# Causal attention of a two-layer block: F32R scores of two heads in the two row halves, and second products in pairs of key tiles

## The chip, the cores and the metric

One core of one Trainium2 chip (trn2) runs the whole program. The metric is device time in microseconds, 2697.65 us before the change as the median of three runs. TensorE is called PE in the rows (its weight loads PEld), VectorE DVE, ScalarE ACT, GpSimd POOL, and SP is the engine that issues most transfers.

## The reference, cut to what matters

Two layers, each `x + attention(norm(x)) * silu(ffn(norm(x)))`. The change touches the attention of the first layer and what feeds it. There x is (2, 2048, 256), with 16 heads of 16 dimensions:

```python
q = (x @ Wq.T).reshape(B, S, H, hd).transpose(0, 2, 1, 3)
...
def body(_, inp):
    qi, ci = inp
    scores = jnp.einsum('bhcd,bhsd->bhcs', qi, k) * scale
    qpos = ci * chunk + jnp.arange(chunk)
    mask = kpos[None, :] <= qpos[:, None]
    scores = jnp.where(mask, scores, jnp.finfo(scores.dtype).min)
    p = jax.nn.softmax(scores, axis=-1)
    return (None, jnp.einsum('bhcs,bhsd->bhcd', p, v))
```

The rest of the program (a mixture of experts, a second attention over windows and a second mixture of experts) is the same code in both kernels.

## The kernel before, in words

The program runs in stages, one block of all engines after the other: constants (`build_constants`), projection (`stage_project`), first attention (`stage_attention`), experts, join, windows.

**Constants.** GpSimd makes an identity, zeros, ones and two mask tiles (L116 to L139), one operation behind the other. The other engines wait for the end of this block.

**Projection** (L220 to L490). Eight chunks of 512 tokens. Per chunk VectorE normalises, TensorE transposes (L466) and multiplies (L457, F32R halves of inputs and weights), and q and k are cut into **three BF16 parts**: ScalarE takes the first (L425), VectorE the rest (L367), ScalarE the second (L430), VectorE the third (L372). SP stores them in DRAM as `qk_parts` (L308), 384 KB for each of four row tiles.

**Attention** (L579 to L912). A group is four heads of one of the two batch entries. There are eight groups, as a loop of three rounds of two, then two more written out. A group has four chunks c of 512 queries and, for chunk c, 4(c + 1) key tiles j of 128 keys; the last four of them lie on the diagonal and cover 512, 384, 256 and 128 queries. The steps, written out by `attention_steps` in one order that all engines follow, are:

- "A" (L721, L724, reduced at L859): the maxima. One product of 128 queries by up to 512 keys of one head, contraction 96 = 6 products of parts times 16 dimensions, into one bank of a ring of three; on the diagonal a mask product of an identity and a mask is added. VectorE reduces the bank to one maximum per query. There are 160 of these in a group. Half of them are made in the group before (in a head of their own for the first group), so the last group has only the other half.
- "M" (L866 to L870) cuts the negated maxima into three BF16 parts, "MT" (L731, L876) turns them into rows, and SP writes these into the operand `qa` of the scores (L691).
- "S" (L774, L777, exponential at L836): scores with keys on the partitions, contraction 99, the three more rows carrying the negated maximum. Two heads fill the two banks of a pair `pss`, and ScalarE takes both banks in one exponential of up to 1024 columns. On the diagonal a mask product is added. There are two `pss` pairs.
- "PV" (L792): the second products of one key tile, four heads in four column tiles of 32, float32 (each runs as two passes, so eight instructions), added up in `acc` over the key tiles. It comes after the scores of the next key tile.
- "COPY" (L844) and "O" (L802, L906, L909): sums to SBUF, four transposes through the ring, division, store.

`weave` (L533) sets the order: after each score it lets in as many maxima steps as keep both in step, so about one to one. The ring's wait in `a_step` is L720:

```python
wait(pe, ring_taken, r + 1 - RING)        # RING = 3
```

and the scores wait until the exponential two before is done (L773). In the head of the stage SP loads q and v, ScalarE issues the loads of k, and GpSimd fills the ones rows of `kb` (L660), clears the table `expert_in` (L665) and scatters the tokens into it (L668).

## Time and profile before

| what | value |
|---|---|
| three runs | 2697.65, 2702.26, 2695.6 us; median 2697.65 |
| the profiled execution | 2692.8 us, and its span is 2692.8 us |
| mean granted TensorE clock | 0.953 |
| projection | up to about 125 us |
| attention, its head | 133 to 224 us |
| attention, eight groups | 224 to 1157 us |
| experts, join, windows | 1157 to 2693 us |

The page has, for each engine, busy time and share of the span, then 40 slices of the span in tenths. A view of windows gives the busy time of each engine in a stretch, the granted clock there (1.00 is 2.4 GHz, 0.50 is 1.2 GHz) and the DMA share. The timeline lists instructions by start and duration, neighbours of one kind merged (x8 is eight of them). The duration of a product holds its latency too; what it keeps TensorE for is the distance from its start to the next start.

### The profile page before, as it was taken

Reading aid. Unit: us, or ns where it says so; the run is one execution under the profiler, and the core shown is the slowest. Engines: PE = TensorE matmul, PEld = TensorE weight load, DVE = VectorE, ACT = ScalarE, POOL = GpSimd, SP = SyncE. Lnnn points to the kernel's source line nnn. Section 1 sums busy time; section 2 is a strip of 40 time slices with the busy share of each in tenths; the row PEclk is TensorE's granted clock in tenths of the full one; section 3 lists DMA queues with packets and bytes.
Section 4 is the critical chain, followed back from the end, with each engine's and each line's share of the span. In section 5 each row is a group of like instructions: output and inputs, shape, how many; then the busy total and the mean of one; then the engine's idle time right before and its main releaser. Section 6 shows DMA issues by size and latency. Waiting matters only on the chain. (4 is left out here: it accounts for less than half of the span.)

```text
span 2692.8 us, 51134 instructions
## 1 busy us (share of the span) xinstructions
PE 2451.3 (91%) x16420; PEld 1589.0 (59%) x16420; DVE 1846.2 (69%) x3682; ACT 1406.8 (52%) x2776; POOL 815.1 (30%) x647
## 2 busy tenths in 40 slices
PE   5648999999999999969977599999999999999999
PEld 4512333333333333358866477777777777777777
DVE  7757877877787777424438476777667767766776
ACT  3404655656565566755634255555555555555554
POOL 1070000000000000014425355554455555444553
PEclk9858999999999999989988699999999999999999
DMA  4574041321404040033257000000000000000000
GB/s 135 191 170 65 5 62 26 41 52 16 61 6 62 6 60 5 7 127 133 102 177 241 18 13 12 11 13 13 13 13 13 9 11 13 13 13 13 13 9 9
DMA packets 189865, 132.85 MB, mean 49 GB/s; under 512 B 99857, under 2 KB 177687, under 8 KB 189712
## 3 DMA queue, kind: packets, MB, share of 16 engines
q1 hardware_dynamic: 160048, 100.06, 15.4%
q10 hardware_dynamic: 24160, 14.16, 2.2%
q0 software_dynamic: 5504, 16.69, 1.7%
q8 instruction: 83, 1.36, 0.2%
q14 instruction: 70, 0.57, 0.1%
HBM read 84.43 MB, written 46.14 MB: 48 GB/s over the span
## 5 line engine op out<-in xcount | busy, mean ns | idle before, releaser
L859 DVE TENSOR_REDUCE a_best<-a_ring 128x1 f32<-128x512 f32 (+3 forms) x1280 | 700.9, 604 | 214.0 <-PE a_ring L721 123.0
L836 ACT ACTIVATE a_probs<-a_pss 128x1024 f32<-128x1024 f32 (+3 forms) x640 | 554.0, 895 | 452.6 <-PE a_pss L777 228.7
L721 PE MATMUL a_ring<-a_kb,a_qa 96*128 96x512 bf16 (+3 forms) x1280 | 453.0, 365 | 67.2 <-DVE a_best L859 32.3
L774 PE MATMUL a_pss<-a_qa,a_kb 99*128 99x512 bf16 (+3 forms) x1280 | 433.9, 353 | 15.6 <-issue 7.2
L1771 ACT ACTIVATE w_probs<-w_pss,w_top 128x256 f32<-128x256 f32 x512 | 239.0, 476 | 379.7 <-DVE w_top L1859 365.0
L1606 POOL TENSOR_TENSOR w_probs<-w_probs,w_inv 128x512 f32<-128x512 f32 x256 | 301.0, 1176 | 395.7 <-DVE w_inv L1865 386.3
L962 POOL TENSOR_TENSOR e_w_r<-e_w,e_w_r 128x1024 fp32r<-128x1024 f32 x28 | 67.0, 2402 | 1032.7 <-ACT e_w_r L1035 1032.7
L1629 PE MATMUL w_psw<-wqkv,w_xr 128*128 128x512 f32 x1152 | 301.5, 398 | 11.6 <-POOL w_xr L1563 11.6
L774 PEld LDWEIGHTS a_pss<-a_qa,a_kb 99*128 99x128 bf16 x1280 | 123.5, 98 | 302.6 <-ACT a_probs L836 224.5
L792 PE MATMUL a_acc<-a_probs,a_vg 128*32 128x512 f32 (+3 forms) x2560 | 299.9, 541 | 0.1
L1669 PE MATMUL w_pss<-w_kd,w_qt 128*128 128x256 f32 x1536 | 278.4, 310 | 0.0
L1859 DVE TENSOR_REDUCE w_top<-w_pss 128x2 f32<-128x512 f32 x256 | 176.8, 691 | 141.5 <-PE w_pss L1669 140.7
L721 PEld LDWEIGHTS a_ring<-a_kb,a_qa 96*128 96x128 bf16 x1280 | 126.4, 99 | 223.9 <-DVE a_best L859 128.6
L1629 PEld LDWEIGHTS w_psw<-wqkv,w_xr 128*128 128x128 f32 x1152 | 205.6, 190 | 47.6 <-POOL w_xr L1563 12.1
L1669 PEld LDWEIGHTS w_pss<-w_kd,w_qt 128*128 128x128 f32 x1536 | 222.0, 195 | 4.1
L1629 PE MATMUL w_psw<-we,w_xr 128*128 128x512 f32 x768 | 204.2, 401 | 0.0
L1710 PE MATMUL w_pso<-w_pt,w_v 128*64 128x128 f32 x2048 | 168.3, 285 | 0.1
L1689 PE MATMUL w_pst<-identity,w_probs 128*128 128x128 f32 x1024 | 155.7, 275 | 0.0
L1629 PEld LDWEIGHTS w_psw<-we,w_xr 128*128 128x128 f32 x768 | 134.9, 188 | 22.9 <-issue 0.2
L1689 PEld LDWEIGHTS w_pst<-identity,w_probs 128*128 128x128 f32 x1024 | 123.6, 140 | 31.2 <-issue 5.7
L1882 DVE SCALAR_TENSOR_TENSOR w_y<-w_psw,coef,w_y 128x256 f32<-128x256 f32 x224 | 108.3, 484 | 42.4 <-PE w_psw L1629 23.2
L1710 PEld LDWEIGHTS w_pso<-w_pt,w_v 128*64 128x64 f32 x2048 | 106.5, 136 | 49.6 <-issue 49.1
(223 smaller groups left out, 3771.2 us busy)
## 6 DMA issues: line engine op xcount, KB each, us to landing
e_w<-in_w SPq DMA_DIRECT2D x16, 1024.0 KB, 7.9
qk_parts<-p_parts SPq DMA_DIRECT2D x32, 384.0 KB, 3.7
a_qa<-qk_parts SPq DMA_DIRECT2D x192, 64.0 KB, 2.5
a_kb<-qk_parts SPq DMA_DIRECT2D x42, 256.0 KB, 9.5
p_xin<-in_x SPq DMA_DIRECT2D x8, 512.0 KB, 5.4
v_rows<-p_vout SPq DMA_DIRECT2D x8, 512.0 KB, 5.1
a_vg<-v_rows SPq DMA_DIRECT2D x32, 128.0 KB, 9.1
expert_in<-zero POOLq DMA_DIRECT2D x16, 256.0 KB, 8.3
```

Source lines behind the costliest of these rows:

```text
L721: ins = pe.matmul(bank[:, 0:keys], qa[u][0:QR, i // TC, h, (i % TC) * P:(i % TC + 1) * P], kb[u][0:QR, h, k * CH:k * CH + keys], start=Tru ...
L774: ins = pe.matmul(pss[idx % 2][:, e, lo:CH], kb[u][0:MR, h, j * P:(j + 1) * P], qa[u][0:MR, c, h, lo:CH], start=True, stop=(j < TC * c))
L792: ins = pe.matmul(acc[32 * h:32 * h + 32, lo:CH], vg[u][:, j, h, :], probs[:, 2 * (pv % 2) + h // 2, h % 2, lo:CH], start=(j == 0), stop=( ...
L836: act.activation(probs[:, idx % 4, :, lo:CH], pss[idx % 2][:, :, lo:CH], ACT.Exp).then_inc(exp_done, 1)
L859: vec.tensor_reduce(best[:, i // TC, h * TC + i % TC, k:k + 1], bank[:, 0:keys], X, ALU.max).then_inc(ring_taken, 1)
L1606: pool.tensor_tensor(probs[:, p % 4, :, :], probs[:, p % 4, :, :], inv[:, :, p:p + 1].to_broadcast([P, 2, 2 * P]), ALU.mult).then_inc(p_re ...
L1629: ins = pe.matmul(psw[bank][:, :], xr[a][:, src, k, :], moving(b, k), start=(m == 0), stop=(m == len(pairs) - 1))
L1669: ins = pe.matmul(scores, qt[a][:, p, :], keys[b][:, p, :, :], start=False, stop=(a, b) == PARTS[-1])
L1689: ins = pe.transpose(pst[r % 2][:, 2 * e + role, :], probs[:, p % 4, e, role * P:(role + 1) * P], keep["identity"][:, :])
L1710: ins = pe.matmul(pso[e * DH:(e + 1) * DH, p % 4, :], v[(u + 1 + role) % 2][:, h * DH:(h + 1) * DH], pt[:, p % 2, 2 * e + role, :], start= ...
L1771: ins = act.activation(probs[:, p % 4, e, :], pss[p % 2][:, e, :], ACT.Exp, bias=top[:, e, p:p + 1], accum_out=rows[:, e, p:p + 1])
L1859: vec.tensor_reduce(top[:, :, p], pss[p % 2][:, :, :], X, ALU.max, negate=True).then_inc(top_ready, 1)
```

## The change

**q and k in two F32R parts.** VectorE's third part and ScalarE's second cast go; `parts` and `qk_parts` become 4 bytes wide with two parts. **Two heads in two row halves.** `qa` and `kb` hold head 2g at partitions 0 to 49 and head 2g + 1 at 64 to 113 (48 rows of products, 2 rows for the maximum), and steps "A" and "S" make two products each. An "A" step takes two banks of the ring, which keeps its three. **Masks.** The maxima's mask becomes two products of 64 rows for each head. The scores' mask goes; GpSimd sets the future's probabilities to zero behind the exponential, and the second product of a diagonal tile waits for that. **Order.** Every second key tile, the second products of two tiles come one behind the other, and `probs` holds four key tiles. The maxima are cut in two parts. The ones rows come by DMA from a constant tile.

```diff
-QR = 6 * HD
-MR = QR + 3
+QR = 3 * HD
+MR = QR + 2
+HALF = P // 2
...
+            for half, low_base in ((0, -HALF), (1, 0)):
+                for part, base in ((slice(0, P), low_base), (slice(0, HALF), HALF * half)):
+                    ch.link(pool.memset(keep["turn_halves"][part, half, :], 0.0))
+                    ch.link(pool.affine_select(out=keep["turn_halves"][part, half, :], in_=keep["turn_halves"][part, half, :],
...
+                    ch.link(pool.affine_select(out=keep["qk_halves"][part, half, :], in_=keep["zero16"][part, :],
...
+            ch.link(pool.memset(keep["ones32"][:, :], 1.0))
...
-                for m in range(4):
-                    rest_of(m)
-                for m in range(4):
-                    third(m)
+                for m in range(4):
+                    vec.wait_ge(high_part, 4 * c + m + 1)
+                    vec.scalar_tensor_tensor(out=parts[:, m, 1, :], in0=psq[m][:, :], scalar=HD ** -0.5 if m < 2 else 1.0,
+                                             in1=parts[:, m, 0, :].bitcast(F32), op0=ALU.mult, op1=ALU.subtract
+                                             ).then_inc(parts_ready, 1)
...
         for n, (c, j) in enumerate(pairs):
-            for h in range(GH):
-                steps.append(("S", c, j, h))
+            for g in range(GH // 2):
+                steps.append(("S", c, j, g))
...
-            if n:
-                pc, pj = pairs[n - 1]
+            for pc, pj in (pairs[n - 2], pairs[n - 1]) if n and n % 2 == 0 else ():
                 steps.append(("PV", pc, pj))
...
+KEPT = 4
...
+    in_ring = {"A": 2, "MT": 1, "O": 1}
...
-        qa = [st.sb(f"qa{u}", [MR, QC, GH, CH], BF16) for u in range(2)]
-        kb = [st.sb(f"kb{u}", [MR, GH, S], BF16) for u in range(2)]
+        qa = [st.sb(f"qa{u}", [P, QC, GH // 2, CH], F32R) for u in range(2)]
+        kb = [st.sb(f"kb{u}", [P, GH // 2, S], F32R) for u in range(2)]
...
-            for u in range(2):
-                pool.memset(kb[u][QR:MR, :, :], 1.0).then_inc(ones_set, 1)
...
+            for g, i, u, order in groups(pool):
+                idx = 0
+                for s in order:
+                    if s[0] == "S":
+                        _, c, j, hp = s
+                        if j >= TC * c:
+                            lo = (j - TC * c) * P
+                            pool.wait_ge(exp_done, primed + g * n_s + idx + 1)
+                            pool.tensor_tensor(spare[:, idx % spare.shape[1]:idx % spare.shape[1] + 1], keep["zero"][:, 0:1], keep["zero"][:, 0:1], ALU.add)
+                            block_probs = probs[:, idx % (KEPT * GH // 2), :, lo:lo + P]
+                            pool.affine_select(out=block_probs, in_=block_probs, compare_op=ALU.is_ge, fill=0.0, base=0,
+                                               pattern=[[0, 2], [1, P]], channel_multiplier=-1).then_inc(future_cleared, 1)
+                        idx += 1
...
+            def masked(bank, e, x, stop):
+
+                return pe.matmul(bank, keep["turn_halves"][half(e, HALF), x, :], keep["qk_halves"][half(e, HALF), x, :],
+                                 start=False, stop=stop)
...
-                wait(pe, ring_taken, r + 1 - RING)
-                ins = pe.matmul(bank[:, 0:keys], qa[u][0:QR, i // TC, h, (i % TC) * P:(i % TC + 1) * P],
-                                kb[u][0:QR, h, k * CH:k * CH + keys], start=True, stop=not diagonal)
+                wait(pe, ring_taken, r + 2 - RING)
+                for e in range(2):
+                    ins = pe.matmul(banks[e][:, 0:keys], qa[u][half(e, QR), i // TC, g, (i % TC) * P:(i % TC + 1) * P],
+                                    kb[u][half(e, QR), g, k * CH:k * CH + keys], start=True, stop=not diagonal)
+                    if not diagonal:
+                        ins.then_inc(ring_full, 1)
                 if diagonal:
-                    ins = pe.matmul(bank[:, keys - P:keys], keep["identity16"][:, :], keep["mask_qk"][:, :],
-                                    start=False, stop=True)
-                ins.then_inc(ring_full, 1)
+                    for x in range(2):
+                        for e in range(2):
+                            ins = masked(banks[e][:, keys - P:keys], e, x, x == 1)
+                            if x == 1:
+                                ins.then_inc(ring_full, 1)
...
+                        pe.wait_ge(exp_done, primed + g * n_s + max(idx - 1, 0))
+                        for e in range(2):
+                            ins = pe.matmul(pss[idx % 2][:, e, lo:CH], kb[u][half(e, MR), hp, j * P:(j + 1) * P],
+                                            qa[u][half(e, MR), c, hp, lo:CH], start=True, stop=True)
+                        ins.then_inc(s_ready, 1)
...
-                        pe.wait_ge(exp_done, primed + g * n_s + 2 * pv + 2)
+                        if j < TC * c:
+                            pe.wait_ge(exp_done, primed + g * n_s + GH // 2 * (pv + 1))
+                        else:
+                            pe.wait_ge(future_cleared, g * n_diagonal + GH // 2 * (j + 1))
...
+                for e in range(2):
+                    vec.wait_ge(ring_full, r + e + 1)
+                    vec.tensor_reduce(best[:, i // TC, e, g * TC + i % TC, k:k + 1], banks[e][:, 0:keys], X, ALU.max
+                                      ).then_inc(ring_taken, 1)
```

## Rows read from the trace of the kernel before

**Rows 1.** The page, part 1: busy us, share of the span, instructions, by engine.

```profile
PE 2451.3 (91%) x16420; PEld 1589.0 (59%) x16420; DVE 1846.2 (69%) x3682; ACT 1406.8 (52%) x2776; POOL 815.1 (30%) x647
```

**Rows 2.** Windows, the attention's groups: length, busy us by engine, clock, DMA share, GB/s.

```profile
225.00:1157.00 932.00, 889.79 (x6171) 336.81 (x6169) 701.46 (x1440) 569.05 (x672) 0.00 (x0) 0.99 0.21 32
```

**Rows 3.** Timeline, TensorE, first score of groups 0 and 2: start, us, what, idle.

```profile
223.60 0.63 PE L774 MATMUL a_pss<-a_qa,a_kb 99*128 99x512 bf16 x1
...
463.58 0.60 PE L774 MATMUL a_pss<-a_qa,a_kb 99*128 99x512 bf16 x1 [3.65 <-issue]
```

**Rows 4.** Timeline, TensorE, from one second product to the next in a full tile.

```profile
630.38 1.06 PE L792 MATMUL a_acc<-a_probs,a_vg 128*32 128x512 f32 x8
631.38 0.39 PE L774 MATMUL a_pss<-a_qa,a_kb 99*128 99x512 bf16 x1
...
632.16 0.38 PE L721 MATMUL a_ring<-a_kb,a_qa 96*128 96x512 bf16 x1
632.38 0.38 PE L774 MATMUL a_pss<-a_qa,a_kb 99*128 99x512 bf16 x1
...
633.30 1.06 PE L792 MATMUL a_acc<-a_probs,a_vg 128*32 128x512 f32 x8
```

**Rows 5.** Timeline, six reductions back to back, and two exponentials of two banks.

```profile
257.10 3.68 DVE L859 TENSOR_REDUCE a_best<-a_ring 128x1 f32<-128x512 f32 x6 [0.77 <-PE a_ring L721]
...
632.44 1.94 ACT L836 ACTIVATE a_probs<-a_pss 128x1024 f32<-128x1024 f32 x2 [1.02 <-PE a_pss L774]
```

**Rows 6.** Waits, 225 to 1157 us: who waited for whom, us in total, times, longest.

```profile
DVE a_best L859 <- PE a_ring L721: 119.4, 168, 4.1
PEld a_ring L721 <- DVE a_best L859: 84.9, 243, 0.8
```

**Rows 7.** Timeline, TensorE, chains of F32R products in the experts' stage.

```profile
1216.69 2.51 PE L1026 MATMUL e_psy<-e_w_r,e_hidden 128*128 128x256 f32 x19
...
1234.66 4.70 PE L1015 MATMUL e_psh<-e_rows_r,e_w_r 128*128 128x512 f32 x20
```

**Rows 8.** Groups by line and shape, reductions: count, busy us, mean ns, idle before.

```profile
L859 DVE TENSOR_REDUCE a_best<-a_ring 128x1 f32<-128x512 f32 x896 | 581.2, 684 | 171.4 <-PE a_ring L721 122.5 <-PE a_ring L724 36.4 <-remote 9.8
...
L859 DVE TENSOR_REDUCE a_best<-a_ring 128x1 f32<-128x384 f32 x128 | 70.5, 551 | 5.0 <-PE a_ring L724 4.0 <-PE a_ring L721 0.5
...
L859 DVE TENSOR_REDUCE a_best<-a_ring 128x1 f32<-128x128 f32 x128 | 36.1, 282 | 31.8 <-PE a_ring L724 26.9 <-remote 4.9
```

**Rows 9.** Timeline, TensorE, a float32 product whose weight load nothing covers.

```profile
2005.04 0.48 PE L1719 MATMUL w_psy<-wout,w_ot 128*128 128x256 f32 x1
```

**Rows 10.** Timeline, GpSimd, the constants' two masks.

```profile
3.05 0.29 POOL L126 TENSOR_SCALAR_AFFINE_SELECT mask_qk<-zero 128x128 bf16<-128x128 bf16 x1
3.49 0.29 POOL L128 TENSOR_SCALAR_AFFINE_SELECT mask_kq<-zero 128x128 bf16<-128x128 bf16 x1
```

**Rows 11.** Windows: before and behind a fall of the clock, one without, the head.

```profile
57.50:60.50 3.00, 1.38 (x11) 1.38 (x12) 2.54 (x12) 1.64 (x7) 0.00 (x0) 1.00 0.91 259
61.00:64.00 3.00, 3.00 (x12) 2.71 (x11) 3.00 (x6) 3.00 (x7) 0.88 (x1) 0.50 0.04 13
...
91.50:94.50 3.00, 1.49 (x13) 1.27 (x11) 2.62 (x17) 1.69 (x3) 0.00 (x0) 1.00 0.98 342
...
160.00:170.00 10.00, 8.92 (x30) 2.50 (x30) 9.34 (x22) 0.00 (x0) 0.51 (x1) 0.50 1.06 322
```

**Rows 12.** Timeline, TensorE, a maxima product of the head at the lower clock.

```profile
188.35 0.61 PE L721 MATMUL a_ring<-a_kb,a_qa 96*128 96x512 bf16 x1 [1.53 <-DVE a_best L859]
```

**Rows 13.** Groups by line, the projection's third part; windows, the projection.

```profile
L372 DVE TENSOR_TENSOR p_parts<-p_rest,p_parts 128x512 bf16<-128x512 f32 x32 | 19.9, 685 | 5.3 <-ACT p_parts L430 5.3
...
50.00:75.00 25.00, 21.21 (x115) 18.33 (x114) 23.60 (x75) 14.61 (x38) 2.09 (x2) 0.93 0.65 211
```

**Rows 14.** Windows, the head's first part, and the group of GpSimd's memset of the ones rows.

```profile
150.00:175.00 25.00, 20.68 (x77) 7.05 (x78) 21.98 (x51) 0.00 (x0) 13.80 (x22) 0.50 0.96 249
...
L660 POOL MEMSET a_kb<- 3x8192 bf16 x2 | 13.8, 6919 | 0.1
```

More of the change, by code:

```diff
@@ L236, in stage_project @@
         xnt = [[st.sb(f"xnt{r}_{u}", [P, KD, CH], F32R) for r in range(2)] for u in range(2)]
-        rest = st.sb("rest", [P, 4, CH])
-        parts = st.sb("parts", [P, 4, 3, CH], BF16)
+        parts = st.sb("parts", [P, 4, 2, CH], F32R)
         vout = st.sb("vout", [P, 2, TC, D])
@@ L420, in back, with high @@
             def back(c, n, u):
-                def first(m):
+                def high(m):
                     act.wait_ge(qk_ready, 4 * c + m + 1)
@@ L425, in first @@
                     act.activation(parts[:, m, 0, :], psq[m][:, :], ACT.Copy, scale=HD ** -0.5 if m < 2 else 1.0
-                                   ).then_inc(first_part, 1)
-                def second(m):
-                    act.wait_ge(rest_ready, 4 * c + m + 1)
-                    act.copy(parts[:, m, 1, :], rest[:, m, :]).then_inc(second_part, 1)
+                                   ).then_inc(high_part, 1)
                 def take_v(t):
@@ L440, in back @@
                 for m in range(4):
-                    first(m)
+                    high(m)
                 for t in range(TC):
                     take_v(t)
-                for m in range(4):
-                    second(m)
             chunks_skewed(act, front, back)
@@ L534, in weave @@
         pairs = [(c, j) for c in range(QC) for j in range(TC * (c + 1))]
-        total = sum(width(*p) for p in pairs) * GH
+        total = sum(width(*p) for p in pairs) * GH // 2
         ahead, steps, done, ahead_done, late = list(ahead), [], 0, 0, []
@@ L544, in advance @@
                 if u[0] == "MT":
-                    late.append([u, 6])
+                    late.append([u, 3])
                 else:
@@ L549, in weave @@
         for n, (c, j) in enumerate(pairs):
-            for h in range(GH):
-                steps.append(("S", c, j, h))
+            for g in range(GH // 2):
+                steps.append(("S", c, j, g))
                 done += width(c, j)
@@ L562, in weave @@
                     steps.append(("COPY", pc))
-                    late.append([("O", pc), 6])
-        c, j = pairs[-1]
-        steps += ahead + [u for u, _ in late] + [("PV", c, j), ("COPY", c), ("O", c)]
+                    late.append([("O", pc), 3])
+        c = pairs[-1][0]
+        steps += ahead + [u for u, _ in late] + [("PV", *p) for p in pairs[-2:]] + [("COPY", c), ("O", c)]
         return steps
@@ L624, in bank_of, with half @@
             return ring[(r_head + u * n_ring + r) % RING]
+        def half(e, rows):
+            return slice(HALF * e, HALF * e + rows)
         primed = 1
@@ L706, in _ @@
                     load(first, 1 - u)
-                for r, s in enumerate(s for s in order if s[0] in in_ring):
+                r = 0
+                for s in order:
                     if s[0] == "MT":
                         store_rows((u + s[1]) % 2, s[2], r_head + g * n_ring + r)
+                    r += in_ring.get(s[0], 0)
             for c in range(2):
@@ L741, in _ @@
                         chunk = s[3] // TC
-                        pe.wait_ge(first_q[chunk], 16 * len(parts_q))
-                    a_step(0, s, r, ring[r % RING])
+                        pe.wait_ge(first_q[chunk], 16 * q_loads)
+                    a_step(0, s, r, [ring[(r + e) % RING] for e in range(2)])
                 if s[0] == "MT":
@@ L875, in take_rows @@
                 wait(vec, m_landed[(c - 2) % QC], landed)
-                vec.tensor_copy(neg_rows[:, c % 2, :], bank[0:3 * GH * TC, 0:P // 2].bitcast(BF16)).then_inc(ring_taken, 1)
-            ch.link(vec.memset(neg_parts[:, :, :], 0.0))
+                vec.tensor_copy(neg_rows[:, c % 2, :], bank[0:2 * M, 0:P]).then_inc(ring_taken, 1)
+            for rest in range(2, P // M):
+                ins = vec.tensor_copy(neg_parts[:, rest, :], keep["zero"][:, 0:M])
+            ch.link(ins)
             r = 0
@@ L882, in _ @@
                 if s[0] == "A":
-                    take(s, r, ring[r % RING])
+                    take(s, r, [ring[(r + e) % RING] for e in range(2)])
                 elif s[0] == "M":
@@ L894, in _ @@
                     if s[0] == "A":
-                        take(s, at, bank)
+                        take(s, at, [bank_of(u, r + e) for e in range(2)])
                     elif s[0] == "M":
@@ L1942, in make_program @@
         }
-        build_constants(nc, keep)
         with ExitStack() as front:
-            keep["xn_all"] = Stage(nc, front).sb("xn_all", [P, NT, D])
+            early = Stage(nc, front)
+            for name in ("turn_halves", "qk_halves"):
+                keep[name] = early.sb(name, [P, 2, P], BF16)
+            keep["ones32"] = early.sb("ones32", [P, CH])
+            keep["xn_all"] = early.sb("xn_all", [P, NT, D])
+            build_constants(nc, keep)
             stage_project(nc, io, keep, dram)
```

169 lines of the change are left out of this document (82 added, 87 removed).

## The prediction

> **What bounds the kernel now.** I read the page first: TensorE is busy 91% of the span, VectorE 69%, ScalarE 52% [rows 1]. That is a mean over stages, so next the stage that the change touches, the attention from 225 us to 1157 us: TensorE 890 of 932 us, VectorE 701, ScalarE 569, GpSimd nothing [rows 2]. Two groups of heads take 463.58 - 223.60 = 240.0 us [rows 3]; later ones are a little slower, and I use **120.5 us a group**.
>
> Inside a group I take one key tile of full width apart. From one second product (L792) to the next is 633.30 - 630.38 = 2.92 us [rows 4]. Neighbouring starts give the prices: a 512-column score product holds TensorE for 0.22 us; from the second product to the next start it is 1.00 us, where 2 x 2 x 512 columns at 2.4 GHz are 0.85. So 8 x 0.22 + 1.00 = 2.76 us of the 2.92 are work; a switch between the two kinds costs 0.1 us behind the second product and, by what is left over, about as much in front of it. The tile is TensorE's. VectorE needs less but is close: six 512-wide reductions, one behind the other, take 3.68 us and one 0.68, so (3.68 - 0.68) / 5 = 0.60 us each [rows 5], 2.4 us for the four of a key tile. ScalarE: two exponentials in 1.94 us [rows 5] with 1.02 for one, 0.92 us each, two per tile. TensorE also waits 85 us on reductions, VectorE 119 us on TensorE [rows 6]: the two already trade turns over the ring of three banks.
>
> **Part 1, cheaper scores.** A score step becomes a pair: two heads in the two row halves, F32R, 512 columns. An F32R product of 512 columns comes every (4.70 - 0.40) / 19 = 0.226 us, one of 256 every (2.51 - 0.28) / 18 = 0.124 us [rows 7]; the price of a pair is not in the trace. Lower bound 0.23 us (both at once, as the four column tiles of L792 do: eight instructions in 1.06 us), upper 0.45 us (one after the other). I take 0.23, because the column tiles are the nearest row. A group has 17408 columns for each of two pairs, for scores and for maxima: 2 x (56 x 0.23 + 8 x (0.17 + 0.12 + 0.12)) = 32 us, where 4 x 17408 x 2 / 2.4 GHz = 58 us are spent now. The score mask (64 products, about 0.06 us each) goes, 3.7 us; the maxima's mask stays, 64 pairs of products of 64 rows, 4 us (bounds 4 and 8). The second products stay at 2 x 17408 x 2 columns, 29 us; with 20 blocks and not 40 the switches fall from 7.6 to 3.8 us. TensorE's own work falls from about 107 to about 73 us a group.
> The Trainium skill, "TensorE: Matmul & The Clock Gate", Part 3, says that products on distinct row groups run at the same time; by it the pair costs 0.23, without it 0.45, and no row here shows row halves.
>
> **Part 2, what it runs into.** VectorE keeps every reduction. In a group, with each width's busy time less the 0.084 us by which neighbours overlap [rows 8]: 112 x 0.60 + 16 x (0.467 + 0.332 + 0.198) = 83.2 us; the splits (three links of five remain, about 0.2 us each), the turned rows and the outputs add 5.5: **88.7 us**. So VectorE is the bound, and every wait of its counts.
> The Trainium skill, "TensorEngine Tiling (Array Packing)", PSUM Bottleneck, speaks against the change in the same way: a faster array leaves the emptying of PSUM as the limit. By that alone the group would be 89 us; the rest is this kernel's order.
>
> *The ring.* There are still three banks, but a maxima step now takes two. It may start when the first reduction of the pair before is done; now it may start with two reductions still ahead of it. From the end of that reduction: about 0.05 us of signal, 0.10 us of weight load that nothing covers (0.48 for a product behind a pause [rows 9] against 0.38 in a stream [rows 4]), 0.39 us of product, 0.04 us of signal: 0.58, against 0.52 that the second reduction covers. That is 0.07 us per full pair; behind a narrow reduction (0.2 to 0.47 us) or with mask products (0.16 more) it is 0.1 to 0.5. Over the 48 plain and 32 masked pairs: 14.6 us a group.
>
> *The second products in pairs.* TensorE is in order: from the last maxima pair (load 0.10, columns 0.21, switch 0.09) through two second products (3 x 0.43 + 0.55 = 1.84), score pair (0.33) and the next maxima pair's 0.43 are 3.0 us, in which VectorE has 1.73 us of work. Stall 1.2 us instead of 0.07. Twelve full blocks, four of 512 + 384 (0.95), four of 256 + 128 (0.15): 18.9 us. Two blocks fewer switches do not help VectorE; the single block of now stalls it by less, since its cover is longer.
>
> *Group end.* No maxima follow the last 512 + 384 block; then come narrow scores, GpSimd's clearing of the last tiles, copy and turn: 5 us of stall.
>
> Sum, at full clock: 88.7 + 14.6 + 18.9 + 5 = **127 us** against 120.5, +6.5.
> ScalarE: 4 x 0.92 = 3.7 us in a period of two full key tiles, which takes 8 x 0.60 + 3 x 0.07 + 1.28 = 6.3 us: covered. GpSimd's clearing after the exponential: 0.29 us for 128 columns [rows 10], 0.3 to 0.5 for 256, plus a small add; two score pairs pass before the product that needs it, so nothing, except at the group end, where it is counted. The wait on it stands in TensorE's queue ahead of the next scores, so if it were late, all would be.
>
> **Part 3, the clock.** In such a period TensorE streams, between two blocks of second products, one maxima and one score pair every 1.27 us; by the busy time of a row, (0.23 + 0.39) / 1.27 = 49%. The granted clock fell to 1.2 GHz behind a stretch with TensorE busy 1.38 of 3 us, and stood behind one with 1.49 [rows 11]. The maxima ahead of the first group ran at 1.2 GHz although TensorE was busy 8.92 of 10 us [rows 11]. So the clock would fall again and again, and come back only by the blocks of second products, 3.6 us without a pause at 1.2 GHz. What it costs there, per period: a 512-column product takes 0.61 us from load to end [rows 12] and not 0.39, so a maxima turn is 1.5 us, three of them 4.5, and the turn over a block is 0.43 + 0.09 + 3.41 + 0.2 + 0.43 = 4.6 us: 9.1 and not 6.3 us. Seventeen periods are 155 us, the extras outside full periods 20 us as at full clock (127 - 17 x 6.3), and some 8 more for turns over narrow reductions: 183 us a group. I take two fifths of the groups' time at the low level (ends: none and all; an estimate, since both the falls and the returns need their stretch to come by): 0.6 x 127 + 0.4 x 183 = **149 us**.
>
> **Part 4, in front.** The projection loses the third part: 32 x 0.60 us of VectorE and a cast of ScalarE [rows 13]. VectorE was busy 23.6 of 25 us there, with 75 instructions, of which a chunk has 36: 11.6 to 12 us a chunk; without 2.4 it is 9.2 to 9.6, and TensorE with 24 x 0.23 + 24 x 0.12 + 8 x 0.11 = 9.4 plus small waits takes over: 9.9. Seven chunks x 1.7 and 2 at the end: -13 us. The stores grow from 384 to 512 KB but in longer rows; as covered as before. The constants gain eleven operations of GpSimd at some 0.4 us apiece (3.49 - 3.05 [rows 10]) in the block that all engines wait for: +4.5 us. The head: VectorE busy 22 of its first 25 us [rows 14]. 13.8 us of GpSimd memset ahead of the table's clearing go [rows 14], so GpSimd's scatter ends earlier; against it stand 43 pairs with turns at 1.2 GHz (0.3 to 0.6 us each). Net 0, bounds -15 and +20. Loads of q and k have the same bytes and number, in rows twice as long; four row stores in place of three, and four stores of ones in SP's queue ahead of the values, lie behind the wait for k.
>
> **Sum.** 7 x (149.4 - 120.5) = +202; the last group, whose second half has no maxima, +12; front -13 + 4.5 + 0: +205. From the profiled execution, 2692.8 us (its span is its time), 2898; the median shown is 4.9 us above it: **2900 us**.
>
> **The rivals.** (a) *The clock holds.* For it: the stretch of 1.49 of 3 us, as busy as I expect here, did not lower it. 7 x 6.5 + 3 - 9 = +40: 2740 us. (b) *The row halves do not run side by side* (the change doesn't do what it says): TensorE is busier, so the clock holds, but each block's stall grows by 0.46 us, 16 blocks, 7.4 us a group: 2790 us. (c) *Faster.* TensorE waits less than I think: if the weight load is pulled ahead of the ring's wait and the mask products add nothing, ring stalls fall to 4 us and the block stalls to 13.4: 111 us a group, 7 x -9.5 - 9 - 5 = -80: 2620 us. It decides as soon as the two stalls together are under 27 us (I have 33.5) and the clock stays up; for it: TensorE's work does fall by a third, and VectorE waits 119 us now that a freer TensorE could serve. (d) *Low clock throughout*: 7 x 62.5 + 25 = +460: 3155 us.
>
> **Chances.** Clock falling often 0.43 (with (d) 0.03 more), (a) 0.20, (b) 0.12, faster (c and between) 0.18, no change 0.04. A measurement can tell 0.3% here, 8 us. Slower 0.78, same 0.04, faster 0.18. The range takes in (a), (b) and most of the clock case's bounds (one tenth to two thirds low), and leaves out the far end of (c) and (d): 2650 to 3060. The forecast case's own range is 2780 to 3060.
>
> **What would show it.** VectorE as busy in the attention as before in us, with waits on the ring's products of about 1.2 us at each block of second products; ring waits of TensorE far above 85 us; a granted clock that swings between 1.0 and 0.5 in the attention; score pairs starting within some ns of each other, 0.23 us from pair to pair; projection chunks of 10 us. A group under 120 us at full clock would show my turns wrong; a steady clock would leave (a).

## The result, and the profile after

| | before | after |
|---|---|---|
| median of the compared runs | 2696.62 us (2693.27 to 2702.26) | 3012.43 us (3007.04 to 3017.72) |
| profiled execution, its span | 2692.8 us | 3006.5 us |
| mean granted clock of the span | 0.953 | 0.849 |

The ratio is 1.1165, with a 95% interval of 1.1142 to 1.1188: slower by 316 us, inside the range, and 112 us above the forecast of 2900. A run over 1.5% above the fastest of its kernel counts as slow and is left out of comparisons; this befell three of e9's six runs and four of e11's seven. The page of the changed kernel, part 1 and the clock's row of part 2, against [rows 1]:

```profile
PE 2563.3 (85%) x16420; PEld 1650.7 (55%) x16420; DVE 1846.2 (61%) x3591; ACT 1392.2 (46%) x2744; POOL 941.8 (31%) x1168
...
PEclk9755978777676777667799877999999999999999
```

VectorE's busy time is the same to a tenth of a us by chance: the projection lost its third parts, and in the seven groups cut out below VectorE shows 15 us more. TensorE has less to do in the attention and still shows 112 us more busy time, since its products ran at the lower clock for much of it: slices 6 to 20, attention but for the end of the last, stand at 6 to 8. To see where the 314 us of the two spans lie, I cut both at the first exponential of a group: the head, seven groups, the last group. Windows of the kernel before (columns as in [rows 2]):

```profile
151.20:225.84 74.64, 43.43 (x139) 13.20 (x140) 46.76 (x98) 0.00 (x0) 39.78 (x48) 0.50 0.55 158
225.84:1061.02 835.18, 796.55 (x5519) 304.96 (x5517) 653.31 (x1344) 498.92 (x588) 0.00 (x0) 0.99 0.23 34
1061.02:1154.20 93.18, 91.23 (x638) 30.72 (x636) 46.63 (x94) 69.51 (x83) 0.00 (x0) 1.00 0.03 7
```

The same windows of the changed kernel:

```profile
144.00:237.26 93.26, 36.95 (x178) 16.80 (x178) 47.12 (x93) 0.00 (x0) 31.47 (x32) 0.50 0.50 133
237.26:1336.44 1099.18, 896.88 (x5518) 353.71 (x5518) 668.47 (x1291) 500.36 (x588) 120.75 (x448) 0.74 0.17 25
1336.44:1466.70 130.26, 108.83 (x596) 38.88 (x596) 47.02 (x88) 69.50 (x83) 16.34 (x62) 0.70 0.02 5
```

The stretch ahead of the head is 7.2 us shorter, the head 18.6 us longer, seven groups 264.0 us longer (157.0 us each and not 119.3), the last group 37.1, and what follows 1539.8 us and not 1538.6: 11.4 + 264.0 + 37.1 + 1.2 = 313.7 us. A clock of 0.74 means that (1 - 0.74) x 2 = 52% of the groups' time was at the lower level. The waits of the attention, 225 to 1467 us, against [rows 6]:

```profile
PEld a_ring L740 <- DVE a_best L883: 363.9, 442, 1.6
DVE a_best L883 <- PE a_ring L740: 228.1, 247, 5.4
DVE a_best L883 <- PE a_ring L730: 193.2, 164, 4.2
PE a_ring L740 <- DVE a_best L883: 190.6, 391, 1.1
```

TensorE and VectorE now wait for each other far more than before (TensorE's weight loads 364 us, where it was 85), and neither is full. The timeline of one stretch at full clock shows both sides of it. TensorE:

```profile
416.71 0.39 PE L740 MATMUL a_ring<-a_kb,a_qa 48*128 48x512 f32 x2
416.94 0.40 PE L797 MATMUL a_pss<-a_qa,a_kb 50*128 50x512 f32 x2
417.89 0.50 PE L740 MATMUL a_ring<-a_kb,a_qa 48*128 48x512 f32 x2 [0.55 <-DVE a_best L883]
418.22 0.39 PE L797 MATMUL a_pss<-a_qa,a_kb 50*128 50x512 f32 x2
419.17 0.50 PE L740 MATMUL a_ring<-a_kb,a_qa 48*128 48x512 f32 x2 [0.55 <-DVE a_best L883]
...
420.44 0.44 PE L740 MATMUL a_ring<-a_kb,a_qa 48*128 48x384 f32 x2 [0.55 <-DVE a_best L883]
420.73 0.29 PE L730 MATMUL a_ring<-qk_halves,turn_halves 64*128 64x128 bf16 x4
420.94 1.92 PE L814 MATMUL a_acc<-a_probs,a_vg 128*32 128x512 f32 x16
422.80 0.44 PE L797 MATMUL a_pss<-a_qa,a_kb 50*128 50x384 f32 x2
```

VectorE in the same stretch:

```profile
417.14 4.93 DVE L883 TENSOR_REDUCE a_best<-a_ring 128x1 f32<-128x512 f32 x8 [2.69 <-PE a_ring L740]
423.51 0.69 DVE L883 TENSOR_REDUCE a_best<-a_ring 128x1 f32<-128x512 f32 x1 [1.44 <-PE a_ring L740]
```

A pair of 512 columns holds TensorE for 416.94 - 416.71 = 0.23 us. A maxima pair comes every 1.28 us, in which TensorE stands 0.55. Then comes the block of sixteen second products, and VectorE, which had run through eight reductions, stands for 1.44 us.

Two maxima turns and a block at the lower clock, which lasted from 599.8 to 606.7 us, VectorE:

```profile
600.87 1.29 DVE L883 TENSOR_REDUCE a_best<-a_ring 128x1 f32<-128x512 f32 x2 [0.28 <-PE a_ring L740]
602.44 1.29 DVE L883 TENSOR_REDUCE a_best<-a_ring 128x1 f32<-128x512 f32 x2 [0.29 <-PE a_ring L740]
607.09 3.12 DVE L883 TENSOR_REDUCE a_best<-a_ring 128x1 f32<-128x384 f32 x5 [3.35 <-PE a_ring L730]
```

A turn takes 602.44 - 600.87 = 1.57 us here, the turn over a block 607.09 - 602.44 = 4.65, and the wait behind the block is 3.35 us. Windows around one fall, a return and the next fall:

```profile
422.40:425.80 3.40, 2.50 (x22) 1.14 (x14) 2.29 (x4) 2.40 (x4) 1.30 (x6) 0.99 0.01 1
425.80:429.20 3.40, 3.40 (x18) 0.59 (x16) 1.57 (x3) 0.20 (x1) 0.85 (x3) 0.50 0.00 0
429.20:432.60 3.40, 2.12 (x20) 1.05 (x16) 1.66 (x3) 2.60 (x4) 1.06 (x4) 1.00 0.01 2
432.60:442.80 10.20, 9.48 (x50) 4.43 (x54) 7.14 (x14) 4.57 (x5) 0.00 (x0) 0.50 0.01 2
```

Here the clock falls behind a stretch with waits (TensorE busy 2.50 of 3.40 us), comes back behind one in which TensorE never stands (a block of second products at 1.2 GHz), and falls again behind the next pauses.

### The profile page after: what moved, and what is told of

It is laid out like the page before. It is cut to its first block and busy times, and to the rows that moved or that the text cites. A ratio compares the mean times of both kernels' runs of the same rounds, so it can differ in the third digit from the quotient of the medians.

```text
span 3006.5 us, 51095 instructions
## 1 busy us (share of the span) xinstructions
PE 2563.3 (85%) x16420; PEld 1650.7 (55%) x16420; DVE 1846.2 (61%) x3591; ACT 1392.2 (46%) x2744; POOL 941.8 (31%) x1168
## 5 line engine op out<-in xcount | busy, mean ns | idle before, releaser
L883 DVE TENSOR_REDUCE a_best<-a_ring 128x1 f32<-128x512 f32 (+3 forms) x1280 | 721.2, 606 | 486.5 <-PE a_ring L740 236.6
L740 PE MATMUL a_ring<-a_kb,a_qa 48*128 48x512 f32 (+3 forms) x1280 | 351.6, 546 | 265.5 <-DVE a_best L883 213.1
L814 PE MATMUL a_acc<-a_probs,a_vg 128*32 128x512 f32 (+3 forms) x2560 | 412.5, 780 | 7.2 <-POOL a_probs L670 7.2
L668 POOL TENSOR_TENSOR a_spare<-zero 128x1 f32<-128x1 f32 x256 | 49.4, 193 | 1130.7 <-ACT a_probs L858 1130.0
L740 PEld LDWEIGHTS a_ring<-a_kb,a_qa 48*128 48x128 f32 x1280 | 151.3, 233 | 452.4 <-DVE a_best L883 396.2
L797 PE MATMUL a_pss<-a_qa,a_kb 50*128 50x512 f32 (+3 forms) x1280 | 317.0, 503 | 23.9 <-ACT a_probs L858 14.2
L797 PEld LDWEIGHTS a_pss<-a_qa,a_kb 50*128 50x128 f32 x1280 | 146.6, 229 | 217.7 <-issue 181.4
L814 PEld LDWEIGHTS a_acc<-a_probs,a_vg 128*32 128x32 f32 x2560 | 85.0, 141 | 205.6 <-issue 146.3
```

Source lines behind the costliest of these rows:

```text
L740: ins = pe.matmul(banks[e][:, 0:keys], qa[u][half(e, QR), i // TC, g, (i % TC) * P:(i % TC + 1) * P], kb[u][half(e, QR), g, k * CH:k * CH ...
L797: ins = pe.matmul(pss[idx % 2][:, e, lo:CH], kb[u][half(e, MR), hp, j * P:(j + 1) * P], qa[u][half(e, MR), c, hp, lo:CH], start=True, stop ...
L814: ins = pe.matmul(acc[32 * h:32 * h + 32, lo:CH], vg[u][:, j, h, :], probs[:, GH // 2 * (pv % KEPT) + h // 2, h % 2, lo:CH], start=(j == 0 ...
L883: vec.tensor_reduce(best[:, i // TC, e, g * TC + i % TC, k:k + 1], banks[e][:, 0:keys], X, ALU.max).then_inc(ring_taken, 1)
```

## The experiments

The theory: a group at full clock takes 127 us, since VectorE waits over each long block and turns with TensorE over three banks; the waits bring the clock down, and the clock makes the rest. The rival of each run is that the part in question costs nothing. Each run stood beside the kernel before on one of four chips, where that took 2671 to 2674 us; the changed kernel was run again in the same way (e5), and the variants are to be compared with that, 3000.5 us. A variant changes the stage of attention alone.

**e1, one tile of second products at a time.**

```diff
-            for pc, pj in (pairs[n - 2], pairs[n - 1]) if n and n % 2 == 0 else ():
+            for pc, pj in (pairs[n - 1],) if n else ():
```

> Undoes one part of the change: the second products of a key tile come alone, behind the scores of the next tile, as before; all else as changed. Theory (VectorE's waits behind TensorE's blocks of second products, and a clock that falls because TensorE is idle between them): the pause between blocks is half as long, VectorE waits about 0.45 us at each block of a full tile and not 1.2 us at each pair, and the clock stays up for more of the time; a group falls from 157 us to about 130 us, the whole to about 2820 us (2760 to 2900). Rival (the pairing is a gain, since it saves half of the switches, and the loss lies elsewhere, in the ring or in GpSimd's clearing): 20 switches more a group at 0.19 us, so 3010 + 30 = 3040 us.

2863.86 us, ratio 1.0704 (1.0669 to 1.0739), clock 0.872. The time is in the theory's range: the pairing costs 137 us in this kernel. The groups got less of it than expected, 143.5 us each at a clock of 0.77 and not about 130.

**e2, each score pair issued twice.** The second issue writes the same numbers into the same bank: work for TensorE and nothing else.

```diff
-                        for e in range(2):
+                        for e in [e for _ in range(2) for e in range(2)]:
                             ins = pe.matmul(pss[idx % 2][:, e, lo:CH], ...
```

> The changed kernel, but each pair of score products is issued twice into the same banks, so that TensorE has 80 x 0.2 us more to do in a group and the result is the same. Theory (the low clock is most of the loss and comes from TensorE's idle time): TensorE is busy for more of the time between blocks, the clock stays up in most of the attention, mean clock of the groups 0.9 or more against 0.74, a group about 133 us against 157, and the kernel gets faster by more work: about 2850 us (2770 to 2930). Rival (the loss is VectorE's waits in the order of the steps, the clock only goes along): each stall at a block grows by 0.23 us, 16 x 0.23 = 4 us a group, 3010 + 30 = 3040 us, and the same clock.

2880.8 us, ratio 1.0777 (1.0738 to 1.0817), clock 0.913. Added work makes the kernel 120 us faster. The seven groups:

```profile
210.15:1228.56 1018.41, 877.10 (x6638) 409.53 (x6638) 667.88 (x1290) 504.63 (x588) 120.68 (x448) 0.88 0.18 27
```

145.5 us a group at 0.88, where the theory had 133 at 0.9 or more. VectorE and ScalarE did what they did without it, and nothing was taken away, so it is the clock that gives the time back. It gives back 120 of the 327 us by which e5 is over the kernel before.

**e3, each maxima product waits for its own bank,** and its mask products stand right behind it, so that the first of a pair need not wait until two banks are free.

```diff
-                wait(pe, ring_taken, r + 2 - RING)
                 for e in range(2):
+                    wait(pe, ring_taken, r + e + 1 - RING)
...
+                    if diagonal:
+                        for x in range(2):
+                            ins = masked(banks[e][:, keys - P:keys], e, x, x == 1)
+                    ins.then_inc(ring_full, 1)
```

> Undoes the two-bank wait alone: each product of a maxima step waits for its own bank of the ring, with its own mask products behind it. Theory (a maxima step that takes two of three banks leaves VectorE's turn uncovered, 14.6 us a group, and makes each block's stall longer): the ring's stalls nearly go, those at blocks fall from 1.2 to about 1.0 us; at full clock 127 - 17 = 110 us a group; with half of the time at the low clock, about 138 us against 157: 2880 us (2820 to 2940). Rival (the first product goes out in time and only the row halves' running together counts): the two heads' products no longer start together and TensorE loses what the halves gave, no gain or a loss: 3010 to 3050 us.

2856.57 us, ratio 1.0686 (1.066 to 1.0713), clock 0.876. The wait for two banks costs 144 us. Of these, 17 lie in the head of the attention, where the first exponential comes at 193.91 us, and at 211.18 in e1, whose head is the changed kernel's; the groups take 143.0 us at 0.78.

**e4, both.**

> Both: second products tile by tile, and a wait for each bank. Theory: VectorE's reductions are the bound with few stalls, TensorE is busy evenly enough for the clock to stay up; 105 to 112 us a group against 120.5 of the kernel before, so faster than before: 2696 - 7 x 12 = about 2610 us (2560 to 2700). Rival (GpSimd's clearing and the load of the F32R weights set the pace): not under the kernel before, 2750 to 2850 us.

2811.32 us, ratio 1.0557 (1.0499 to 1.0615), clock 0.889: the theory missed, by 200 us. The two repairs overlap (137 + 144, together 189 us). The groups say what is left over:

```profile
195.53:1144.81 949.28, 882.61 (x5520) 384.01 (x5519) 649.40 (x1290) 496.17 (x588) 123.25 (x451) 0.81 0.20 31
```

135.6 us a group at 0.81. They range from 129.3 us at 0.87 to 146.9 at 0.71; a line through the seven gives 120 us at full clock and 0.32 us more for each us at the lower level (an estimate; the same line for e5 gives 128 and 0.36). So at full clock this order would, by that line, be as fast as the kernel before (119.3 us), and no faster, though TensorE's work fell by a third by the prediction's count. Its timeline at full clock shows part of the reason, TensorE:

```profile
292.18 1.06 PE L810 MATMUL a_acc<-a_probs,a_vg 128*32 128x512 f32 x8
...
293.99 0.40 PE L740 MATMUL a_ring<-a_kb,a_qa 48*128 48x512 f32 x1
294.69 0.50 PE L740 MATMUL a_ring<-a_kb,a_qa 48*128 48x512 f32 x1 [0.31 <-DVE a_best L879]
295.12 1.07 PE L810 MATMUL a_acc<-a_probs,a_vg 128*32 128x512 f32 x8
```

VectorE in the same stretch, and a window of 12 us:

```profile
293.95 2.48 DVE L879 TENSOR_REDUCE a_best<-a_ring 128x1 f32<-128x512 f32 x4
...
299.58 3.17 DVE L879 TENSOR_REDUCE a_best<-a_ring 128x1 f32<-128x512 f32 x6 [0.54 <-PE a_ring L740]
...
292.00:304.00 12.00, 11.26 (x79) 4.90 (x78) 10.01 (x22) 6.94 (x8) 0.00 (x0) 1.00 0.01 3
```

A key tile takes 295.12 - 292.18 = 2.94 us. VectorE does not stand in this one: four reductions of 0.60 us and 0.54 us of splits are as long. But the last maxima product waits 0.31 us for a bank, the block begins only behind it, and the two products of that pair (293.99 and 294.69) no longer start together. Over the 12 us VectorE stands 2.0 us in all, 0.24 to 0.70 at a time, behind blocks and mask products. How much each of these costs was not measured.

**e5, the changed kernel again.**

> The changed kernel as it is, beside the variants, to have a second reading of it. Its first execution had VectorE and TensorE standing for 10.5, 5.9 and 3.1 us at a time in the head of the attention, and its first exponential at 237 us, where the variant with the scores twice, which has the same head, had it at 210 us. Theory (that was of the one execution, the clock is of the kernel): first exponential at 205 to 215 us, mean clock between 0.84 and 0.86, groups of 148 to 163 us, 2970 to 3000 us in all. Rival (the long groups too were of the one execution): groups under 145 us and below 2930 us.

3000.53 us, ratio 1.1231 (1.1212 to 1.1249), clock 0.85; the first exponential at 211.25 us, groups of 150 to 164 us. The clock belongs to the kernel. The head is 26 us shorter than in the first execution, but so is that of e12, whose front is the kernel before's: its first exponential comes at 201.16 us and not at 225.84. So the change moves it by 11.4 us in the one pair of executions and by 10.1 in the other.

**e6, the second product of a tile in two halves of 256 columns,** one behind each score pair, with e3's waits.

```diff
+                if g == 1 and n >= 1:
+                    steps.append(("PH", *pairs[n - 1]))
+                if g == 0 and n >= 2:
+                    pc, pj = pairs[n - 2]
+                    steps.append(("PV", pc, pj))
...
+                        part = (lo, CH // 2) if s[0] == "PH" else (max(lo, CH // 2), CH)
```

> The second product of a key tile in two halves of 256 columns, one behind each score pair, on top of the waits for one bank. Theory (VectorE starves for what TensorE does in one piece between two maxima pairs, and the clock falls because of the pauses that follow): the pieces shrink from two tiles (2.0 us with the switch) to half a tile (0.5 us and two switches), a key tile needs 2 x (0.24 + 0.34 + 0.5 + 0.2) = 2.6 us of TensorE, with VectorE at 2.4; a group of 105 to 115 us at full clock, clock over 0.93, 2590 to 2680 us in all. Rival (row-half pairs and switches cost TensorE more than that, and the low clock stays): two switches for each half tile make it 3.0 us or more, groups of 125 to 145 us, 2740 to 2870 us.

2721.85 us, ratio 1.0193 (1.0147 to 1.0239), clock 0.9: the fastest variant, 279 us below e5, and still slower than the kernel before. It lies between the two ranges: the theory was right about the key tile, the rival about the low clock. TensorE in the wide tiles:

```profile
300.68 0.64 PE L816 MATMUL a_acc<-a_probs,a_vg 128*32 128x256 f32 x8
301.25 0.50 PE L796 MATMUL a_pss<-a_qa,a_kb 50*128 50x512 f32 x2
301.58 0.44 PE L743 MATMUL a_ring<-a_kb,a_qa 48*128 48x512 f32 x2
301.95 0.64 PE L816 MATMUL a_acc<-a_probs,a_vg 128*32 128x256 f32 x8
```

VectorE there:

```profile
300.78 6.83 DVE L888 TENSOR_REDUCE a_best<-a_ring 128x1 f32<-128x512 f32 x12 [0.26 <-PE a_ring L743]
307.80 3.33 DVE L888 TENSOR_REDUCE a_best<-a_ring 128x1 f32<-128x512 f32 x6 [0.18 <-PE a_ring L743]
```

Half a tile takes 301.95 - 300.68 = 1.27 us, a key tile 2.54, and VectorE runs through twelve reductions without a wait: the theory's 2.6. But near every border of a group the clock fell, and then stayed low for 20 to 58 us. Windows of the 8 us ahead of a fall (at 320.6 us), of wide tiles at full clock, and of the start of the last group at the lower one:

```profile
312.00:316.00 4.00, 2.88 (x40) 1.12 (x40) 1.29 (x2) 1.88 (x4) 2.18 (x8) 1.00 0.00 0
316.00:320.00 4.00, 3.60 (x21) 2.13 (x21) 3.08 (x7) 1.73 (x3) 0.55 (x2) 1.00 0.54 137
...
1000.00:1060.00 60.00, 57.17 (x586) 27.54 (x578) 48.65 (x100) 37.65 (x44) 8.78 (x33) 1.00 0.03 7
1062.00:1094.00 32.00, 31.99 (x194) 12.95 (x195) 18.73 (x36) 14.29 (x17) 4.67 (x17) 0.50 0.02 5
```

**e7 and e8, filler on top of e4:** every score pair twice, and only those of diagonal tiles twice.

```diff
-                        for e in range(2):
+                        for e in [e for _ in range(2 if j >= TC * c else 1) for e in range(2)]:
```

> One tile of second products at a time, waits for one bank, and each score pair issued twice: the filler on top of the better order. At full clock the order without the filler took 120 us a group, and each us at the low level added 0.3 us. Theory (what is left over before is the low clock, and a fuller TensorE keeps it up): clock over 0.95; the filler adds 56 x 0.24 + 8 x 0.35 = 16 us of TensorE to a group, of which the pauses take up to a half: groups of 122 to 134 us, 2700 to 2800 us in all. Rival (the level does not follow how full TensorE is): clock 0.87 to 0.90, groups over 140 us, 2850 to 2930 us.

> As the one-bank, one-tile order, with the filler only in the score pairs of the key tiles on the diagonal (32 of the 80 pairs of a group, 512 to 128 columns): the clock fell in that order at 325, 339, 359 and 452 us, near the borders of groups, where these tiles are. Theory (the fall begins in the narrow tiles at the borders): clock 0.92 or more, groups near 125 us, 2690 to 2760 us. Rival (it falls in the wide part as well, and the filler only costs): clock 0.87 to 0.90, 2800 to 2850 us.

e7: 2784.07 us, ratio 1.0419 (1.0401 to 1.0436), clock 0.938. e8: 2757.28 us, ratio 1.0314 (1.0297 to 1.0331), clock 0.919. Both times are in the theory's ranges, the clocks just under them: work that computes nothing new makes e4 27 and 54 us faster. The full dose has the higher clock and the longer groups (133.1 us at 0.93, against 131.3 at 0.88): it costs TensorE time that this order doesn't have.

**e9 to e11, filler on top of e6.** e9 issues the diagonal tiles' score pairs twice; e10 puts pairs of products where TensorE stands at the end of a group (two ahead of the last second product, four ahead of the turn of the sums); e11 does both.

```diff
+            def filler(u, into, n):
+                for e in n * [0, 1]:
+                    pe.matmul(into[:, e, 0:CH], kb[1 - u][half(e, QR), 0, 0:P], qa[1 - u][half(e, QR), 0, 0, 0:CH],
+                              start=True, stop=True)
...
+                        if next_seen and c == QC - 1:
+                            filler(u, pss[idx % 2], 4)
                         pe.wait_ge(sums_copied, primed + g * QC + c + 1)
```

> The half-tile pieces, and the score pairs of diagonal tiles issued twice. The half-tile order stood at a full clock in the wide tiles (a key tile in 2.52 us, VectorE without a pause) and fell at every border of a group (320.6, 440.1, 576.6, 689.3 us and so on), for 26 to 55 us each time; by its groups, 110 us are left at full clock. Theory (the narrow tiles at the border pull the level down): low time of a group under 20 us, clock over 0.93, 2620 to 2690 us in all. Rival (it falls at the border all the same and the filler only costs, 32 x 0.2 = 6 us a group at most): 2700 to 2760 us.

> The half-tile pieces, and filler only where TensorE pauses at the end of a group: two product pairs (512 columns) ahead of the last second product, which waits 0.5 us for GpSimd, and four ahead of the turn of the sums, which waits 0.8 us for ScalarE's copy. Theory (these two pauses, 312 to 316 us with TensorE busy 2.9 of 4 us, are what brings the level down): low time of a group under 20 us, 2620 to 2690 us. Rival (the narrow tiles before and behind them matter more, so the level falls a few us later): within 15 us of the half-tile order, 2705 to 2740 us.

> Both fillers. Theory (each removes a part of the pauses at a border): low time of a group under 10 us, groups of 110 to 114 us, 2600 to 2660 us in all, faster than the kernel before by 1% or more. Rival (falls have other causes, and both fillers cost): 2690 to 2760 us.

e9: 2777.74 us (2739.66 to 2801.8), ratio 1.041 (1.0366 to 1.0454); its three lowest took 2739.66 to 2768.11. e10: 2755.9 us (2734.09 to 2773.43), ratio 1.0329 (1.0297 to 1.0361). e11: 2754.35 us (2713.61 to 2767.98), ratio 1.0173 (1.0145 to 1.02); its three lowest took 2713.61 to 2745.2, like e6's. The theories missed in all three; e9 lies at the upper end of its rival, e10 above its own. The filler of e10 filled the pauses it was aimed at, and the clock fell all the same. Windows of e10 ahead of three falls:

```profile
552.78:559.78 7.00, 6.79 (x55) 3.60 (x51) 3.51 (x8) 2.73 (x5) 1.65 (x7) 1.00 0.34 86
675.66:682.66 7.00, 3.76 (x36) 2.03 (x37) 0.81 (x3) 0.97 (x2) 1.02 (x4) 1.00 0.33 75
...
962.38:969.38 7.00, 6.63 (x64) 3.05 (x66) 5.41 (x10) 4.83 (x7) 2.54 (x10) 1.00 0.01 2
```

Only the second has a long pause: TensorE stood 3.2 of 7 us at the turn of the loop of two groups, as the kernel before does for 3.65 us [rows 3], and there too the clock is at 0.50 behind it. What brings the clock down in the other two stays open; I had taken the pauses of TensorE in the rows for the whole cause, and that is not shown. The runs of these kernels also scatter: e9's by 2.2%, e10's by 1.4%, those of the kernel before by 0.4%. In e9's profile one of the seven groups took 154 us at a clock of 0.67, while the others took 119 to 128.

**e12, the pairing alone in the kernel before,** with eight buffers for the probabilities of four tiles.

```diff
-        probs = st.sb("probs", [P, 4, 2, CH])
+        probs = st.sb("probs", [P, 8, 2, CH])
...
-            if n:
-                pc, pj = pairs[n - 1]
+            for pc, pj in (pairs[n - 2], pairs[n - 1]) if n and n % 2 == 0 else ():
                 steps.append(("PV", pc, pj))
```

> The kernel before with one part of the change alone: the second products of two key tiles side by side, with probabilities of four tiles kept. Scores, maxima, masks and projection stay as they were, so TensorE stays the bound of a key tile (2.76 of 2.92 us). Theory (pairing costs only where VectorE is the bound; where TensorE is, the saved switches count): 20 blocks less with 0.19 us of switching each are 3.8 us a group, a block of 2.0 us takes VectorE 1.8 us of full banks to cover, clock over 0.94, 2630 to 2665 us in all, a ratio of 0.985 to 0.998. Rival (the block alone lengthens the turns or brings the clock down, as in the changed kernel): VectorE's and ScalarE's waits behind a block come back as waits of TensorE, 1 to 2 us per block of two tiles, 16 blocks a group, or clock under 0.92: 2750 us or more.

2693.52 us, ratio 1.0079 (1.0066 to 1.0093), clock 0.958: slower by 0.8%, and neither theory nor rival. The seven groups, and the wait that took the gain:

```profile
201.16:1047.68 846.52, 792.52 (x5519) 317.40 (x5517) 645.79 (x1344) 501.75 (x588) 8.84 (x9) 0.99 0.23 36
```

```profile
PEld a_ring L720 <- DVE a_best L858: 125.5, 330, 1.3
```

The clock stays at 0.99, as TensorE has no room to stand. 120.9 us a group and not 119.3: the busy time falls by only 0.6 us (113.2 against 113.8), and the ring's wait grows (125.5 us from 250 to 1100 us, where it was 81.6 in the kernel before). The 119.3 are of another chip; beside the kernel before on the same chip e12 takes 20.4 us more, 2.5 a group. So the long block costs about 2 us a group where TensorE is the bound, and 17, clock included, in the changed kernel (137 us over eight groups).

## Why the prediction was right, and where it was off

**Part 1.** The lower bound held: a pair holds TensorE for 0.23 us, one product's time, and its two products start 3 or 4 ns apart in most pairs. With that rival (b), row halves one after the other, falls. Behind a wait a pair is recorded with 0.50 us where it has 0.39 in a stream: 0.11 us of load that nothing covers, against 0.10 taken from [rows 9].

**Part 2.** VectorE's turn per pair was put at 2 x 0.60 + 0.07 = 1.27 us; the timeline has 1.28 and 1.27. The wait behind a full block was put at 1.2 us and is 1.44: 0.2 us short. The period was put at 6.3 us; VectorE's runs begin 423.51 - 417.14 = 6.37 us apart, with one pair of 384 columns among them. GpSimd's clearing was put at nothing away from the group's end, and TensorE's second products waited 7.2 us for it in the whole stage, as the page's part 5 has it:

```profile
L814 PE MATMUL a_acc<-a_probs,a_vg 128*32 128x512 f32 (+3 forms) x2560 | 412.5, 780 | 7.2 <-POOL a_probs L670 7.2
```

The group at full clock, 127 us, was not measured. The line through e5's groups gives 128, but from groups that spent 44 to 64% of their time at the lower level, so it reaches far. VectorE, whose work in a group is fixed, gives another reading. Sums over all stretches of the changed kernel's seven groups at the lower clock, then over all at the full one:

```profile
sum 577.61, PE 527.58 PEld 195.91 DVE 314.62 ACT 187.34 POOL 48.51; mean PE 7.13 PEld 2.65 DVE 4.25 ACT 2.53 POOL 0.66
sum 521.57, PE 369.30 PEld 157.79 DVE 353.85 ACT 313.02 POOL 72.25; mean PE 4.99 PEld 2.13 DVE 4.78 ACT 4.23 POOL 0.98
```

VectorE is busy 54% of the one and 68% of the other; with its 95.5 us a group that is 175 and 141 us. The 141 is a high estimate, since waits behind a block at 1.2 GHz end when the clock is back. Between 128 and 141 it stays open how much of the loss is waits at full clock. e1 and e3 take away one of the two stalls each, and each was worth some 140 us, clock included.

**Part 3.** That the clock would fall again and again was right, and its share too small: I took two fifths of the groups' time at the lower level, and it was 52%. Two terms of the low price can be read off: a turn takes 1.57 us where 1.5 stood, and the turn over a block 4.65 where 4.6 stood. By the prediction's own two prices, 0.48 x 127 + 0.52 x 183 = 156 us a group, and 157.0 was measured. The groups are 7 x (157.0 - 149.4) = 53 of the 112 us by which the sum was short. Some of this agreement may be luck: with VectorE's 141 and 175 us, two fifths would have given 155, and the short term would be the group at full clock. Nor does the busy share tell when the clock falls, as the prediction read it from [rows 11]: it fell behind 2.50 of 3.40 us as well. That a part of the loss is the clock alone is shown by e2, e7 and e8, where TensorE only got more to do. Rival (a), a clock that holds, was wrong for this kernel, and (d) was too far.

**The last group** was put at +12 us and took +37. This step failed: its clock was left out. Its window shows 0.70, and 60% of 130 us at a price of 0.36 us each are 28.

**Part 4.** The constants: TensorE's first product came at 20.48 and not 16.29 us, +4.2 against +4.5. From chunk to chunk of the projection ScalarE's first cast moved from 11.74 to 10.20 us, against a forecast of 11.7 to 9.9: seven chunks gave 10.8 us, and the whole stretch ahead of the head 7.2, forecast 8.5. The head was put at 0 with bounds of -15 and +20. It took +18.6, and this step failed too. Both executions of the first pair have long stands of VectorE in the head (up to 10.5 us after, up to 4.9 us before), which e5 and e12 don't have; without them the head takes 67.6 us in e5 and 48.2 in e12, 19.4 apart. The head ran at 0.50 in both. VectorE in e12's head, then in e5's:

```profile
180.92 20.69 DVE L858 TENSOR_REDUCE a_best<-a_ring 128x1 f32<-128x512 f32 x39 [0.21 <-PE a_ring L720]
...
202.09 1.29 DVE L883 TENSOR_REDUCE a_best<-a_ring 128x1 f32<-128x512 f32 x2 [0.28 <-PE a_ring L740]
203.67 1.29 DVE L883 TENSOR_REDUCE a_best<-a_ring 128x1 f32<-128x512 f32 x2 [0.28 <-PE a_ring L740]
```

The kernel before reduces without a stand, 0.53 us each; the changed one takes 1.58 us for every pair. With a wait for each bank (e3) 17 of the 19 us go. So the turns cost what the prediction had for them (43 pairs, 0.3 to 0.6 us each); the gain from GpSimd's memset, set against them, is what did not come: e12's VectorE shows that the head did not wait for it.

Together: 53 from the groups, 25 from the last group, 20 from the front (11.4 where -8.5 stood), and the rest from 120.5 us a group taken for the kernel before, where the cut at the exponentials gives 119.3 (8), the tail, the medians, and 2898 + 4.9, which is 2903 and was written as 2900.

**Rival (c), faster,** had its condition, both stalls together under 27 us and a clock that stays up. e4 came near the first (by its line, 120 - 88.7 - 5 = 26 us) and not the second. e6 shows that the room is there: in the wide tiles 2.54 us against 2.92 [rows 4]. No version that was run beats the kernel before.

## What to carry to other kernels

In this kernel, making one engine's work cheaper where it trades turns with another moved the bound to the other, and the saved time turned into pauses; the longer a piece that the first engine did in one go, the longer the second starved, so the pieces have to shrink with the work. Before a TensorE-bound stage is lightened, look whether it still fills TensorE: here two thirds of the work, by the prediction's count, took 32% more time in the groups. Look also at stretches that have only one of the steps, such as the head: a wait that hides elsewhere stands bare there. A filler of products that changes no result is a cheap experiment to tell the clock's share from the waits'.

## What had not been expected

Added products made the kernel faster: 120 us in e2, 54 us in e8. The clock also fell where the rows show TensorE busy for 6.79 of 7.00 us, and stood for 60 us where it was busy for 57.17; busy time holds the latency of each product, and the share of it does not tell which stretch falls. And once low in e6, it stayed so for 32 us with TensorE busy for 31.99 of them, at the start of the last group. What decides between the two is not shown by these runs.
